# Experts by position in one block: norms by tile, scale and shift on turned columns, half of the last product made early

## The reference, cut to what matters

```python
def _L1_ffn_ref(x, ln_g, ln_b, attn_w, attn_b, gate_w, fc1_w, fc1_b, fc2_w, fc2_b, next_w, next_b):
    ...
    normed = (xf - mu) / jnp.sqrt(var + 1e-05) * ln_g + ln_b
    x_attn = normed @ attn_w.T + attn_b + xf
    ...
    t = b * s // (MICRO_BATCHES * e)
    tok = x_attn.reshape(MICRO_BATCHES, e, t, d)
    h = jnp.einsum('meti,ehi->meth', tok, fc1_w) + fc1_b[None, :, None, :]
    h = jax.nn.gelu(h, approximate=False)
    y = jnp.einsum('meth,edh->metd', h, fc2_w) + fc2_b[None, :, None, :]
    yf = y.reshape(b * s, d)
    out = jax.nn.gelu(yf @ next_w.T + next_b, approximate=False)
    return out.reshape(b, s, d)
...
x = x + _L1_ffn_ref(_layernorm(x, axis=-1)[None], L1_ffn_ln_g, ...)
```

## Time and profile before

| | us |
|---|---|
| median of 3 runs | 2386.29 (2381.55 to 2393.45) |
| the profiled execution | 2388.08 |
| its span in the trace | 2386.3 |
| PE busy | 1992.9 (84% of the span) |
| DVE, ACT, POOL busy | 989.6, 489.1, 344.2 |
| mean granted TensorE clock, as a share of full speed | 0.915 |

### The profile page before, as it was taken

How to read it: one execution, slowest core, us unless ns; L and a number is a source line. 1 busy time by engine, 2 the same in 40 slices (tenths; PEclk the granted TensorE clock), 3 DMA queues, 4 the chain that set the end, 5 groups by cost and what they waited for, 6 DMA issues and landing times. The chain is left out here.

```text
span 2386.3 us, 28543 instructions
## 1 busy us (share of the span) xinstructions
PE 1992.9 (84%) x9076; PEld 1039.4 (44%) x9112; DVE 989.6 (41%) x2936; ACT 489.1 (20%) x1236; POOL 344.2 (14%) x363
## 2 busy tenths in 40 slices
PE   8798967999579698869886859869779999949995
PEld 4354545777233233323332323324334444438883
DVE  6463533000367786778677830136420111121111
ACT  0152521111213350125012402217110000010000
POOL 0000001333146204520462000000000000010002
PEclk9899988999789799879987979989889999969997
DMA  0202048994465206520556059943360220078892
GB/s 25 80 1 89 1 184 302 329 326 162 106 194 158 73 1 208 143 75 1 150 149 204 12 202 387 387 140 140 108 219 0 75 75 0 0 288 308 310 333 86
DMA packets 181873, 359.79 MB, mean 151 GB/s; under 512 B 29008, under 2 KB 38496, under 8 KB 181728
## 3 DMA queue, kind: packets, MB, share of 16 engines
q1 hardware_dynamic: 156992, 283.54, 33.4%
q0 software_dynamic: 24736, 74.34, 10.7%
HBM read 335.22 MB, written 22.62 MB: 150 GB/s over the span
## 5 line engine op out<-in xcount | busy, mean ns | idle before, releaser
L1257 POOL DMA_INDIRECT w<-xl_d,src_i x228 | 231.4, 1015 | 414.9 <-DMA xl_d<-XL 263.1
L926 PEld LDWEIGHTS ps<-tokT,w 128*128 128x128 f32 x2304 | 263.8, 194 | 11.4 <-issue 6.7
L926 PE MATMUL ps<-tokT,w 128*128 128x128 f32 x2304 | 264.6, 278 | 3.5 <-DVE tokT L1017 3.5
L1370 PE MATMUL ps<-w,oht 128*128 x660 | 199.9, 406 | 49.6 <-issue 44.9
L1461 ACT ACTIVATE w<-ps 128x512 f32<-128x512 f32 x114 | 65.6, 596 | 375.5 <-PE ps L1375 120.4
L1370 PEld LDWEIGHTS ps<-w,oht 128*128 128x128 bf16 x684 | 61.1, 101 | 185.5 <-issue 163.2
L1375 PE MATMUL ps<-w,ident 128*128 128x512 f32 x228 | 128.9, 646 | 7.2 <-issue 7.2
L1070 POOL DMA_INDIRECT spread_d<-N,slot x12 | 11.8, 984 | 769.0 <-DVE slot L998 766.0
L940 PE MATMUL ps<-w,O 128*128 128x512 f32 x256 | 111.2, 592 | 0.0
L1598 DVE SCALAR_TENSOR_TENSOR w<-w,att 128x512 f32<-128x512 f32 x114 | 77.8, 682 | 64.8 <-issue 32.9
L1621 DVE SCALAR_TENSOR_TENSOR M<-pen,L,M 128x128 bf16 x228 | 78.2, 343 | 41.7 <-issue 35.4
(11 more groups left out here) (444 smaller groups left out, 3057.6 us busy)
## 6 DMA issues: line engine op xcount, KB each, us to landing
w<-L_ffn_W SPq DMA_DIRECT2D x16, 2048.0 KB, 13.2
w<-L_ffn_W SPq DMA_DIRECT2D x8, 4096.0 KB
w<-fc1T SPq DMA_DIRECT2D x32, 1024.0 KB, 14.3
w<-fc2T SPq DMA_DIRECT2D x32, 1024.0 KB, 14.3
w<-L_ffn_w_gate SPq DMA_DIRECT2D x20, 1024.0 KB, 10.6
w<-L_ffn_w_up SPq DMA_DIRECT2D x20, 1024.0 KB, 13.6
w<-L_ffn_w_down SPq DMA_DIRECT2D x10, 2048.0 KB
w<-L_ffn_w SPq DMA_DIRECT2D x8, 2048.0 KB, 12.6
```

The costliest lines, as they stand in the source:

```text
L926: m = pe.matmul(k.ps[:, 1 + (q * ins + i) % 4, s * P:(s + 1) * P], self.W1[u][i][:, f, (q * T + s) * P:(q * T + s + 1) * P], self.tokT[:, ...
L1257: gp.indirect_dma_start(self.G[:, i % FAR_AHEAD, :], None, k.xl_d, bass.IndirectOffsetOnAxis(ap=k.src_i[:, i:i + 1].bitcast(U32), axis=0)) ...
L1370: m = pe.matmul(bank, self.oht[:, i * P:(i + 1) * P], self.XP[:, q].rearrange("p t n -> p (t n)")[:, bass.ds(at, D)], start=False, stop=(q ...
```

## The change

All five blocks become one, with semaphores of their own.

- SP: column forms of gain and shift (`pos_g`, `pos_b`, 128x4 each), `attn_b`, `attn_wT`, `b1`, then W2 of pair 0 with no wait, then b2. When the attention product is done it loads `next_wT` into the buffer of `attn_wT`. The loads of the later pairs are freed as before, by quarters. `next_b` (nb) is loaded ahead of pair 3's W2, into a part of b2 that is read out by then (b2[:, 2, :]).
- First norm: DVE takes the second norm's statistics of a tile of N as soon as it is scaled, between the scalings. All four columns of NT are copied by ACT.
- Second norm: only scaled on rows; gain and shift are applied as the turned columns are copied out of PSUM, f = 0 and 2 by ACT, 1 and 3 by DVE. It is turned into banks 4 to 7.
- The attention product signals each feature tile; DVE's two additions for it run while the next is made.
- Loop: h is turned one quarter behind the first product (`turn_hidden(j, q - 1)` after `first(j, q)`); y of the pair before is turned after quarter 0, now in bank 6.
- The last product is made by token tiles. Tiles 0 and 2 hold tokens of experts 0 to 3 alone, so they are made inside pair 3 (`last(0)` after quarter 1, `last(1)` after quarter 2, both in bank 7), with nb, gelu and the addition to X following on DVE and ACT. Tiles 1 and 3 remain for the end.
- In the layer before (`gains_in`), two small loads that nothing read are no longer issued for the last of its three sub-layers.

```diff
-            sp.dma_start(self.gain_c[:, j, :], k.i[("gat_gc", "gat_bc")[j]][l]).then_inc(self.gain_cols.sem, 16)
+            if l < self.LAYERS - 1:
+                sp.dma_start(self.gain_c[:, j, :], k.i[("gat_gc", "gat_bc")[j]][l]).then_inc(self.gain_cols.sem, 16)
...
-                sp.wait_ge(k.stored[0].sem, k.stored[0].at(32))
...
+                sp.wait_ge(mixed.sem, mixed.at(T))
+                sp.dma_start(W[:], rows_of(i_["next_wT"])).then_inc(k.loaded.sem, 16)
+                for j in range(1, PAIRS):
+                    for q in range(T):
+                        sp.wait_ge(hid.sem, hid.at(T * (j - 1) + q + 1))
+                        x.load_first(sp, j, q)
+                    if j == PAIRS - 1:
+                        sp.wait_ge(biased.sem, biased.at(j))
+                        sp.dma_start(nb, bcast(i_["L1_ffn_next_b"])).then_inc(k.loaded.sem, 16)
+                    for q in range(T):
+                        sp.wait_ge(summed.sem, summed.at(T * (j - 1) + q + 1))
+                        x.load_second(sp, j, q)
...
+            @block.tensor
+                for j in range(PAIRS):
+                    for q in range(T):
+                        first(j, q)
+                        if q:
+                            turn_hidden(j, q - 1)
+                        elif j:
+                            turn_y(j - 1)
+                        if j == PAIRS - 1 and q in (1, 2):
+                            if q == 1:
+                                pe.wait_ge(k.loaded.sem, k.loaded.at(96))
+                            last(q - 1, 2 * (q - 1), 7)
+                    turn_hidden(j, T - 1)
+                    if j:
+                        pe.wait_ge(y_out.sem, y_out.at(j))
+                    for s in range(HT):
...
+                turn_y(PAIRS - 1)
+                last(2, 1, 7)
+                last(3, 3, 0)
...
+            @block.scalar
+                for g in range(2):
+                    a.wait_ge(stats.sem, stats.at(g + 1))
+                    a.activation(rstd[:, g, :], mv[:, g, :, 1], ACT.Sqrt, bias=k.eps[:, 0:1]).then_inc(root.sem, 1)
+                    if g:
+                        a.wait_ge(k.loaded.sem, k.loaded.at(80))
+                    for f in range(0, T, 1 + g):
+                        a.wait_ge(turned.sem, turned.at(T * g + f + 1))
+                        if g == 0:
+                            a.activation(k.NT[:, f, :], k.ps[:, f, :], ACT.Copy).then_inc(cols_a.sem, 1)
+                        else:
+                            a.activation(N2T[:, f, :], k.ps[:, T + f, :], ACT.Identity, bias=gc[:, 1, f:f + 1],
+                                         scale=gc[:, 0, f:f + 1]).then_inc(cols_a.sem, 1)
...
+            @block.vector
+                    for t in range(T):
+                        v.tensor_scalar(rows[g][:, t, :], (k.X, k.N)[g][:, t, :], mv[:, g, t, 0:1], rstd[:, g, t:t + 1],
+                                        ALU.subtract, ALU.mult).then_inc(normed.sem, 1)
+                        if g == 0 and t:
+                            v.wait_ge(normed.sem, normed.at(t))
+                            v.bn_stats(st[:, 1, t - 1, :], k.N[:, t - 1, :])
...
+                def last_add(n, bank):
+                    v.wait_ge(last_out.sem, last_out.at(n + 1))
+                    if n == 0:
+                        v.wait_ge(k.loaded.sem, k.loaded.at(112))
+                    if n >= 2:
+                        add_to_x(n - 2)
+                    v.tensor_tensor(o[n % 2], k.ps[:, bank, :], nb, ALU.add).then_inc(last_sum.sem, 1)
```

More of the change, by code:

```diff
@@ L1810, in positional_ffn @@
     with ExitStack() as c:
[L1811 to L1825, removed]
+        (stats, root, normed, turned, cols_a, cols_v, mixed, shifted, hid, hid_out, hid_turned, gelued, summed, biased,
+         y_turned, y_out, last_out, last_sum, last_gelu) = signals(
+             c, k, "pos_stats", "pos_root", "pos_normed", "pos_turned", "pos_cols_a", "pos_cols_v", "mixed", "shifted",
+             "hidden", "hidden_out", "hidden_turned", "gelued", "pos_summed", "biased", "y_turned", "y_out", "last_out",
+             "last_sum", "last_gelu")
@@ L1826, in gains, with _ @@
+        hT = k.N[:].rearrange("p a (b n) -> p (a b) n", n=P)
+        W1, W2, YT = x.W1, x.W2, k.NT
+        rows = (k.N, XA)
+        with k.nc.Block() as block:
+            @block.sync
+            def _(sp):
+                for j, m in enumerate(("pos_g", "pos_b")):
+                    sp.dma_start(gc[:, j, :], i_[m]).then_inc(k.loaded.sem, 16)
                 sp.dma_start(ab[:], i_["attn_b"]).then_inc(k.loaded.sem, 16)
-                sp.dma_start(nb[:], bcast(i_["L1_ffn_next_b"])).then_inc(k.loaded.sem, 16)
@@ L1828, in gains @@
                 sp.dma_start(W[:], rows_of(i_["attn_wT"])).then_inc(k.loaded.sem, 16)
-                sp.wait_ge(k.stored[0].sem, k.stored[0].at(32))
                 sp.dma_start(b1[:], i_["fc1b"].rearrange("e p m -> p e m")).then_inc(k.loaded.sem, 16)
                 x.load_second(sp, 0)
[L1833 to L1846, removed]
-                            v.scalar_tensor_tensor(by_expert(XA[:, t, :], m), by_token(k.ps[:, t, :], m),
-                                                   ab[:, t:t + 1], by_token(k.NT[:, t, :], m), ALU.add, ALU.add)
@@ L1959, in positional_ffn @@
-        W, o = XA, sb(c, k, "o", [P, T, D])
-        with nc.Block() as block:
+                for e in range(EXPERTS):
+                    sp.dma_start(b2[e % 2 * SL:(e % 2 + 1) * SL, e // 2, :], bcast(i_["L1_ffn_fc2_b"][e], SL)
+                                 ).then_inc(k.valued.sem, 16)
+                sp.wait_ge(mixed.sem, mixed.at(T))
[10 more added lines that the diff above has]
+                        x.load_second(sp, j, q)
@@ new lines, in _ @@
+                pe.wait_ge(k.loaded.sem, k.loaded.at(80))
+                for t in range(T):
+                    if t == 0:
+                        pe.wait_ge(cols_a.sem, cols_a.at(T))
+                    for f in range(T):
+                        if t == 0:
+                            here = (cols_a, cols_v)[f % 2]
+                            pe.wait_ge(here.sem, here.at((T if f % 2 == 0 else 0) + f // 2 + 1))
+                        m = pe.matmul(k.ps[:, t, :], W[:, f, t * P:(t + 1) * P], N2T[:, f, :], start=(f == 0),
+                                      stop=(f == T - 1))
+                    m.then_inc(mixed.sem, 1)
@@ new lines, in first @@
+                def first(j, q):
+                    for u in range(2):
+                        pe.wait_ge(k.pos_first[u][q].sem, k.pos_first[u][q].at(16 * (j + 1)))
+                    if j:
+                        pe.wait_ge(hid_out.sem, hid_out.at(T * (j - 1) + q + 1))
+                    for f in range(T):
+                        if j == q == 0:
+                            pe.wait_ge(shifted.sem, shifted.at(f + 1 if f else T))
+                        for u in range(2):
+                            e = 2 * j + u
+                            m = pe.matmul(k.ps[u * SL:(u + 1) * SL, q, :], XA[:, f, e * SL:(e + 1) * SL],
+                                          W1[u][:, f, q * 512:(q + 1) * 512], start=(f == 0), stop=(f == T - 1))
+                    m.then_inc(hid.sem, 1)
```

244 lines of the change are left out of this document (127 added, 117 removed).

## The result

The changed kernel took 2354.77 us (median of four runs, 2353.02 to 2358.46), the kernel before 2386.64 in the runs beside it: a ratio of 0.986, 95% interval 0.9836 to 0.9884. The forecast was 2351, with 2342 to 2360. The profiled execution took 2353.58 us, its span is 2351.9 at a mean granted clock of 0.922 (before 0.915).

What follows compares the result with a forecast made beforehand. The expert weight stream's start and what follows its last landing were taken to bound the kernel. Earlier landing (1535.0) plus a 15.7 us tail ends the stage at 1550.7 instead of 1586.06: 35.4 us off 2386.3, forecast 2351, range 2342 to 2360.

Steps and rivals of the forecast that it cites:

- The front: Norms and attention product ahead of the expert loop: first expert product at 1396.4 instead of 1420.23, 23.8 us earlier.
- the 1.0 that I took for lost clock: Second norm's transposes and attention product: half clock after PE's rest loses between 0 and 2.5 us; 1.0 taken.
- the front is slower: Rival, 15 in 100: half clock lasts into the attention product or fc1b lands after 1380; 2353 to 2356 us.
- The stream's issue: Expert weight loads of pairs 1 to 3: first issued at 1399.9 instead of 1426.00, 26.1 us earlier.
- the two bounds: Last landing of the weight stream: 1535.4 by issue, 1533.8 by bytes at 387 GB/s; 1535.0 taken, nearer the first.
- the stream starts behind a backlog: Rival, 10 in 100: b2's 1 MB takes 5.9 us instead of 2.7, queue full until 1405; 2353 to 2355 us.
- Inside the loop: Expert loop: a pair falls from 34.8 to about 32 us; two early tiles, 7 us, hidden with 1.6 us margin.
- PE as the bound in pair 3: Rival, 10 in 100: the early last-product tiles are not covered in pair 3, up to 7 us show; 2358 us.
- turning by quarters: Expert loop: h's transposes fit between first products, so the pile-up falls from 5.64 to about 3.2 us, 2.4 less.
- The tail: From the last weight landing to the stage's end: 15.7 us, with two tiles of the last product instead of four.
- The gain passes through whole: Behind the layer: the next block starts after it with no load issued ahead, so all 35.4 us are kept.
- the rival of a half clock in the loop: Rival, 3 in 100: PE resting for DMA falls to 1.2 GHz in pairs 2 and 3; slower, 2414 us.

Runs made afterwards that it cites:

- the kernel with the clock kept ahead of sage: Changed kernel plus 44 products of zeros on PE behind the transposes of the sage layer's norm; 2271.39 us, ratio 0.9844 to the kernel before.
- the kernel without b2: Changed kernel with b2 filled with zeros by GpSimd instead of loaded, leaving out the second product's bias; layer 184.5 us, whole time 2297.92 us.
- the two longer fronts: Changed kernel with 12 or 24 products of zeros behind the attention product's first tile (2.6 or 5.2 us); last quarter starts at 168.9 or 171.3, layer 187.2 or 188.0.
- the biases as products: Changed kernel with b2 and nb loaded as nine rows and added by PE products instead of broadcast loads; 2268.74 us, ratio 0.9839 to the kernel before.
- the kernel with the tile in pair 2: Changed kernel with biases added by PE products, one early last-product tile moved to pair 2, one bias product moved behind the last turning; 2268.14 us, ratio 0.9829.
- the experiment with W2's loads moved: Kernel before with only pair 0's W2 loads moved from the first norm's block to the attention product's block; layer 209.8 us against 219.0.

## Why the prediction was right, and what it missed

**The front** came as laid out. The square root did wait behind ACT's copies (it stands right behind them, at 1368.08). The attention product started at 12.8 us, forecast 13.1; the first expert product at 27.8, forecast 29.0. The 1.2 us are mostly the 1.0 that I took for lost clock: the product had its full 13.97. Both ends of that bound are real, though: the second profile of the kernel before lost 2.1 us there, and one profile with the changed front (the kernel with the clock kept ahead of sage) 2.0 us, in the second transposes and the product:

```profile
1293.00:1299.00 6.00, 5.62 (x19) 4.30 (x20) 2.84 (x5) 2.73 (x3) 0.00 (x0) 0.55 1.05 393
```

So the rival "the front is slower" does come up in some executions. It costs nothing there, because the backlog ahead of the stream covers it.

**The stream's issue** moved by 27.1 us, forecast 26.1, and its last piece was taken up by PE at 169.7, forecast 167.6. This is the mis-sized term, and the choice between the two bounds was wrong with it: the issue was taken as the limit, and the bytes are. The bound by bytes gave 1533.8 because it put b2's 1 MB at 387 GB/s; the windows show 239 GB/s over 6 us there, with the engines full, which loses 2.3 us. The rival "the stream starts behind a backlog" named this and gave it 10 in 100. It applies at 2.6 to 2.9 us, as the kernel without b2 and the two longer fronts agree. I took its row for a stretch that started empty, and put the 236 GB/s of the earlier trace rows down to that. For the old place that is true: from 1421 to 1429 the engines were at a share of 0.59 and moved 170 GB/s, so b2 went as fast as SP issued it, and that row could not show what it does to full engines.

**Inside the loop** the forecast held: PE waits for weights from pair 2, the clock was 1.00 over 1405 to 1530 through waits of up to 1.8 us, and the two early tiles are hidden, with a wait of 1.63 us left where 1.6 was forecast. That the margin is the same does not confirm the landings: PE's work in pair 3 is set off by landings too, so both came some 2.1 us later than forecast. DVE waited 7.14 us for nb and began to add it 148.1 us into the layer, forecast 145.9 (1513.3), and the last quarter's weights came 2.1 us late. PE as the bound in pair 3 was a near rival: it decides as soon as the turning is put back (the last quarter 4.2 us later, 2.5 of it clock) or the stream is 3 us earlier (the biases as products). What the prediction gave to turning by quarters, 2.4 us a pair, left out that the clock holds.

**The tail** is 16.1 us from the last quarter's start to the last addition to X, forecast 15.7, and 1.7 more when the clock falls.

**"The gain passes through whole"** is the step that did not hold. The layer gained 32.6 us (35.4 forecast), but the sage layer's front lost 3.4 and the rest 2.2 us, means over the two profiles of each kernel. For the front, the windows show that it is clock. The 2.2 us are no property of the change: the same code takes 323.8 and 324.2 us behind two variants of the changed layer, as it did before. Why a shorter layer 94 us earlier should shift the front's clock is not shown; the same sage code behind the kernel with the tile in pair 2 has 154.3. That the forecast is only 3.8 us off (1.0 by the profiled span) is helped by a start of the layer that came 3 to 8 us earlier, for which I have no cause; the two small loads that the change drops are not it, as the experiment with W2's loads moved shows. By the layer and what follows it alone the gain is 26.2 us in these two profiles.

The Trainium skill, "TensorE: Matmul & The Clock Gate", section "HAM oscillation — how this bites in real kernels", tells of a kernel that waits longer for its transfers than it computes between them, and falls to the half clock at every tile. The loop here is another case: its waits of 1.6 to 1.8 us lie between bursts of 3.65 us and left the clock at 1.00, so no run here tests what the page describes, and it gives the rival of a half clock in the loop no support. Where the clock did fall, PE had turned tiles with rests of 0.8 to 1.5 us (in the tail, and in the loop with the turning put back) or rested 11 to 12 us (ahead of the gate's product).

## What to carry to other kernels

Where a stream of weights sets the end of a loop, price what is queued ahead of it by the rate at which its own kind of load moves, not by the stream's: here eight loads that copy a row to 64 partitions each filled the engines at some 60% of the rate, while one that copies a row to all 128 ran at the full rate. A row read from engines that stood half empty doesn't show that rate. Work that is hidden behind a transfer is free only up to the margin at the last piece; read that margin first, then decide how much to move, and move the rest one stage earlier. And expect a few microseconds at places where PE has just done sparse work to come and go with the clock, between executions as well as between kernels, before explaining them by the edit.

## What was not expected of the hardware

- Eight loads that each spread one row of 2 KB over 64 partitions, 1 MB in all, kept the DMA engines at a share of 1.06 to 1.08 and moved 232 to 241 GB/s, against 387 for the weights. Not loading them brought the last piece 2.9 us forward. A load that spreads such a row over 128 partitions passed at 387 GB/s.
- With one stage unchanged, the same 32 products took 13.97 or 16.09 us in two executions of one kernel, and the last two tiles 7.13 or 8.83 in two of the other.
- The order of the same transposes changed the clock in the loop: one quarter behind the first products it stayed at 1.00, all four in a row with rests of 1.49 and 1.01 us were followed by 0.57 over 6 us, and 64 products took 16.49 us instead of 13.95.
- 44 small products of zeros, 9.66 us of PE's time in a place where it rested, were followed by work that took 4.6 us less in one kernel, and gained nothing in another.
